# Cross attention's unit becomes a head pair with all four query tiles, and the left keys multiply a block-diagonal V

## The reference

```python
x = x + tanh(g_xattn[0]) * xattn(layernorm(x), ctx_1024, ctx_1024, mask)   # x: 2 x 512 x 256, ctx: 2 x 1024 x 256
# xattn: 16 heads of 64
dots = einsum('bhid,bhjd->bhij', heads(q @ Wq), heads(k @ Wk)) * 64 ** -0.5
dots = where(mask, -finfo.max, dots)                    # True is masked
out = einsum('bhij,bhjd->bhid', softmax(dots), heads(v @ Wv)) @ Wo + bo
x = x + tanh(g_ffn[0]) * ffn(layernorm(x))
# ffn: 8 experts of 256 x 256, gelu; each row takes the result of the expert with the largest gate
```

## Time and profile before

| | us |
|---|---|
| median of 3 runs | 241.98 (241.69 to 244.35) |
| the profiled execution | 242.49 |
| its span, first to last instruction | 240.7 |
| batch 0: first scores to Wo projection | 38.10 to 101.29 |
| batch 1: first scores to Wo projection | 127.29 to 180.84 |

### The profile page before, as it was taken

One profiled execution on the slowest core, in us unless ns is written; L12 is line 12 of the kernel. 1 busy time (PEld: TensorE's weight loads), 2 busy tenths in 40 slices (PEclk: granted clock), 3 DMA queues, 4 the chain that ended last, 5 costly groups with the idle time before them and its releaser, 6 DMA issues.

```text
span 240.7 us, 4102 instructions
## 1 busy us (share of the span) xinstructions
PE 217.7 (90%) x1316; PEld 145.8 (61%) x1316; DVE 134.3 (56%) x537; ACT 112.5 (47%) x386; POOL 90.5 (38%) x96
## 2 busy tenths in 40 slices
PE   0499999999999999999999799999999999959960
PEld 0334394456555544488894356565568899948950
DVE  0797424678878722325227777788883435345520
ACT  2101443877887721301234868778844034525420
POOL 5000710555544591000001657755483000776450
PEclk9999999999999999999999999999999999999995
DMA  3990658999990000091000100240000000235011
GB/s 113 365 394 26 183 234 252 331 317 313 233 316 13 0 3 1 0 297 52 3 1 0 46 3 22 62 143 0 0 3 1 3 0 0 82 112 162 31 49 30
DMA packets 21250, 25.24 MB, mean 105 GB/s; under 512 B 1875, under 2 KB 19805, under 8 KB 21088
## 3 DMA queue, kind: packets, MB, share of 16 engines
q1 hardware_dynamic: 19200, 22.58, 30.4%
q0 software_dynamic: 1152, 2.12, 2.6%
q10 hardware_dynamic: 864, 0.15, 0.3%
HBM read 14.21 MB, written 11.68 MB: 108 GB/s over the span
## 4 chain that ended last, share of the span: by engine, by line
PE 68%; issue 12%; DMA 6%; DVE 5%; POOL 4%; ACT 3%; POOLq 0%; DVEq 0%
PE s_bank L1491 11%; PE s_bank L1531 10%; PE bank L1560 8%; PE bank L1563 7%; PE bank L1450 6%; PE bank L1544 5%; PE s_bank L1588 4%; PE s_bank L1776 3%; PE bank L1545 3%; PE bank L1548 3%; DMA oT<-sorted_rows 2%; PE bank L1571 2%; PE bank L1787 2%; DMA rows<-in_x_dram 2%; POOL sorted_rows L537 2%
## 5 line engine op out<-in xcount | busy, mean ns | idle before, releaser
L563 POOL TENSOR_TENSOR probs<-probs,r_col 128x768 f32<-128x768 f32 x32 | 46.9, 1466 | 86.5 <-DVE r_col L1148 86.5
L717 ACT ACTIVATE probs<-probs,negm_run 128x192 f32<-128x192 f32 x128 | 57.1, 448 | 19.5 <-DVE negm_run L1173 19.5
L1173 DVE CUSTOM_DVE_ANT_0 probs<-s_bank,maskneg 128x192 f32<-128x192 f32 x128 | 39.5, 348 | 8.6 <-PE s_bank L1531 8.6
L1491 PE MATMUL s_bank<-xnT,wq_sb 128*128 128x512 f32 x64 | 31.7, 644 | 1.2 <-ACT xnT L670 0.6
L1182 DVE COPY pT<-bank 128x512 f32<-128x512 f32 x32 | 22.1, 691 | 13.6 <-PE bank L1545 13.6
L1531 PE MATMUL s_bank<-k_sb,q_sb 64*128 64x192 f32 x256 | 29.5, 349 | 0.0
L1450 PE MATMUL bank<-wo_sb,oT 128*128 128x256 f32 x128 | 28.7, 380 | 0.0
L1450 PEld LDWEIGHTS bank<-wo_sb,oT 128*128 128x128 f32 x128 | 23.9, 190 | 3.9 <-issue 0.9
L1531 PEld LDWEIGHTS s_bank<-k_sb,q_sb 64*128 64x128 f32 x256 | 20.0, 186 | 9.0 <-issue 7.9
L717 ACT ACTIVATION_READ_ACCUMULATOR probs<-probs,negm_run 128x1 f32 x128 | 24.1, 188 | 0.0
L1491 PEld LDWEIGHTS s_bank<-xnT,wq_sb 128*128 128x128 f32 x64 | 12.6, 206 | 16.4 <-issue 15.0
(11 more groups left out here) (141 smaller groups left out, 288.5 us busy)
## 6 DMA issues: line engine op xcount, KB each, us to landing
sorted_rows<-empty_row SPq DMA_DIRECT2D x8, 1040.0 KB, 13.3
oT<-in_L_ffn_W_dram SPq DMA_DIRECT2D x1, 2048.0 KB, 17.6
q_sb<-in_L_ffn_W_dram SPq DMA_DIRECT2D x1, 2048.0 KB, 8.4
oT<-sorted_rows SPq DMA_DIRECT2D x1, 1040.0 KB, 6.6
oT<-sorted_rows SPq DMA_DIRECT2D x8, 130.0 KB, 2.2
rows<-in_x_dram SPq DMA_DIRECT2D x2, 512.0 KB, 7.8
wq_sb<-in_L_xattn_Wq_dram SPq DMA_DIRECT2D x1, 1024.0 KB, 8.3
mask_sb<-in_mask_BxSxS_bk_dram SPq DMA_DIRECT2D x2, 512.0 KB, 9.9
```

The lines of the kernel that those rows point to most:

```text
L563: nc.gpsimd.tensor_tensor(part, part, r_col[:, u % PB].rearrange("p i h -> p (i h)") .unsqueeze(2).broadcast_to([P, 4, keys]), ALU.mult).t ...
L717: last = nc.scalar.activation(window_part(u, i, h), window_part(u, i, h), ACT.Exp, bias=negm_run[at], scale=-1.0, accum_out=l_run[at])
L1173: nc.vector.tensor_tensor_reduce(window_part(u, i, h), s_bank[u % 2][:, h, i * CK:i * CK + WK], maskneg[:, q, 0:WK], -SCALE, LARGEST, ALU. ...
L1491: last = nc.tensor.matmul(bank[m % 4], wq_sb[:, c, m * P:(m + 1) * P], xnT[:, c, b * N:(b + 1) * N], start=(c == 0), stop=(c == DC - 1))
```

## The change

The unit on PE, for everything behind the scores, is now a head pair with all four query tiles, eight a batch. PE does both scores of the next pair, then `values(m - 1)`, then twelve transposes, to banks 4 and 6 (head 0's wide and the left block of either half) and 5 (head 1's wide of both). The left half of `v_sb` is zeroed once by POOL, and the left V is copied to its two diagonal blocks (64 x 64 for a pair): one matmul of 128 x 128 against 512 columns then does both heads' left keys, and four of 128 x 64 against 256 columns add the wide ones, all in bank 7. `pT` holds one pair. DVE copies banks 4 and 6 and takes bank 7 in one copy; ACT copies bank 5, whole. Scatters follow multiplies 1 (two), 3 and 5. In batch 1's last pair `values(6)` comes ahead of the filled-in chunks. DVE takes half of the left V copy, which was all ACT's. The branch for other masks changes only in line numbers and counts.

```diff
+        pair_pT = pT[:].rearrange("p a h k n -> p (a h k n)")[:, 0:3 * 2 * CK].rearrange("p (s t n) -> p s t n", s=3, t=2)
+        pair_bank = (4, 6, 5)
...
-            return (v_sb[:, 0, 0:512], v_sb[:, 0, 512:1024], v_sb[:, 1, 0:512])[v], bank[(4, 6, 7)[v]]
+            return v_sb[:, 0, v * 512:(v + 1) * 512], bank[(4, 6)[v]]
+        v_left = v_sb[:, 1, :].rearrange("p (m h d) -> p m h d", h=2, d=DH)
+        def left_v_dst(h):
+            return v_left[head_rows[h], :, h, :], bank[7][head_rows[h], :].rearrange("p (m d) -> p m d", d=DH)
...
+            nc.gpsimd.memset(v_sb[:, 1, :], 0.0).then_inc(left_zero, 1)
...
-                if u == 0:
+            def sort_first_batch(u, first_scatter=1):
+                if u == first_scatter:
                     pool.wait_ge(s_empty, 16 * CH)
                     pool.wait_ge(place_ready, 1)
                     for q in range(2):
                         scatter(q)
-                elif u in (4, 6):
-                    scatter(u // 2)
+                elif u in (first_scatter + 2, first_scatter + 4):
+                    scatter((u - first_scatter) // 2 + 1)
...
-            def window_pT(b, u):
-                act.wait_ge(first.ptrans_ready, b * 2 * PER + (2 * u + 2))
-                if u >= 2:
-                    act.wait_ge(first.o_ready, b * PER + (u - 1))
-                nc.scalar.copy(pT[:, u % 2, 1, 0, :], bank[5][:, 0:2 * P]).then_inc(first.pT_act, 1)
+            def pair_pT_wide(b, m):
+                act.wait_ge(first.ptrans_ready, 3 * (b * M + m) + 3)
+                if m >= 1:
+                    act.wait_ge(first.o_ready, b * M + m)
+                nc.scalar.copy(pair_pT[:, 2].rearrange("p t n -> p (t n)"), bank[pair_bank[2]]).then_inc(first.pT_act, 1)
...
-                for u in range(AHEAD):
+                act.wait_ge(first.v_ps, b * 3 + 1)
+                nc.scalar.copy(*window_v_dst(0)).then_inc(first.v_act, 1)
+                for u in range(2):
                     window_exp(b, u)
-                    act.wait_ge(first.v_ps, b * 3 + (2 * u + 1))
-                    nc.scalar.copy(*window_v_dst(2 * u)).then_inc(first.v_act, 1)
-                for u in range(PER):
-                    if u + AHEAD < PER:
-                        window_exp(b, u + AHEAD, (0,))
+                act.wait_ge(first.v_ps, b * 3 + 3)
+                nc.scalar.copy(*left_v_dst(0)).then_inc(first.v_act, 1)
+                for m in range(M):
+                    if m + 1 < M:
+                        for u in (2 * m + 2, 2 * m + 3):
+                            window_exp(b, u)
                     else:
-                        fill(u + AHEAD - PER)
-                    window_pT(b, u)
-                    if u + AHEAD < PER:
-                        window_exp(b, u + AHEAD, (1,))
-                fill(2)
-                fill(3)
+                        fill(0)
+                    pair_pT_wide(b, m)
+                for k in range(1, 4):
+                    fill(k)
...
-            def window_pT(b, u):
-                dve.wait_ge(first.ptrans_ready, b * 2 * PER + (2 * u + 1))
-                if u >= 2:
-                    dve.wait_ge(first.o_ready, b * PER + (u - 1))
-                nc.vector.tensor_copy(pT[:, u % 2, 0].rearrange("p t n -> p (t n)"), bank[4]).then_inc(first.pT_dve, 1)
+            def pair_pT_left(b, m, j):
+                dve.wait_ge(first.ptrans_ready, 3 * (b * M + m) + 1 + j)
+                if m >= 1:
+                    dve.wait_ge(first.o_ready, b * M + m)
+                nc.vector.tensor_copy(pair_pT[:, j].rearrange("p t n -> p (t n)"), bank[pair_bank[j]]).then_inc(first.pT_dve, 1)
+            def pair_o(b, m):
+                dve.wait_ge(first.o_ready, b * M + m + 1)
+                nc.vector.tensor_copy(oT[:, b, m, :], bank[7]).then_inc(first.o_dve, 1)
...
-                for u in range(AHEAD):
+                for u in range(2):
                     window_max(b, u)
-                    also(f"v{u}")
-                    if u == 0:
-                        dve.wait_ge(first.v_ps, b * 3 + 2)
-                        nc.vector.tensor_copy(*window_v_dst(1)).then_inc(first.v_dve, 1)
-                        take_sum(first, b * PER, 0, l_run)
-                for u in range(PER):
-                    ahead = u + AHEAD
-                    if ahead < PER:
-                        window_max(b, ahead, (0,))
-                        take_sum(first, b * PER, ahead - 1, l_run)
-                        window_max(b, ahead, (1,))
+                also("v0")
+                take_sum(first, g, 0, l_run)
+                dve.wait_ge(first.v_ps, b * 3 + 2)
+                nc.vector.tensor_copy(*window_v_dst(1)).then_inc(first.v_dve, 1)
+                also("v1")
+                take_sum(first, g, 1, l_run)
+                dve.wait_ge(first.v_ps, b * 3 + 3)
+                nc.vector.tensor_copy(*left_v_dst(1)).then_inc(first.v_dve, 1)
+                for m in range(M):
+                    if m + 1 < M:
+                        for u in (2 * m + 2, 2 * m + 3):
+                            window_max(b, u)
                     else:
-                        if ahead == PER:
-                            take_sum(first, b * PER, PER - 1, l_run)
-                        fill(ahead - PER)
-                    window_pT(b, u)
-                    if u >= 1:
-                        take_o(first, b * PER, u - 1, b)
-                    also(u)
+                        fill(0)
+                    if m >= 1:
+                        pair_o(b, m - 1)
+                    if m + 1 < M:
+                        take_sum(first, g, 2 * m + 2, l_run)
+                    for j in range(2):
+                        pair_pT_left(b, m, j)
+                    if m + 1 < M:
+                        take_sum(first, g, 2 * m + 3, l_run)
+                    also(m)
+                fill(1)
+                pair_o(b, M - 1)
                 fill(2)
-                take_o(first, b * PER, PER - 1, b)
                 fill(3)
...
-                if k == 2:
-                    first_rows(range(5, 7))
+                if k == 0:
+                    first_rows(range(2, 3))
...
-                if where in (PER - 5, PER - 4):
-                    first_rows(range(where + 5 - PER, where + 6 - PER))
-                elif where == PER - 2:
-                    first_rows(range(2, 5))
+                if where == M - 2:
+                    first_rows(range(2))
+                elif where == M - 1:
+                    first_rows(range(3, 6))
...
-                def transposes(u):
-                    pe.wait_ge(first.pn_ready, g + (u + 1))
-                    if u >= 1:
-                        pe.wait_ge(first.pT_act, g + u)
-                        pe.wait_ge(first.pT_dve, g + u)
-                    tiles = window_probs(u).rearrange("p (i t k) -> p i t k", i=2, t=3)
-                    for i in range(2):
-                        nc.tensor.transpose(bank[4][:, i * P:(i + 1) * P], tiles[:, i, 0], ident[:])
-                        last = nc.tensor.transpose(bank[4][:, CK + i * P:CK + (i + 1) * P], tiles[:, i, 1], ident[:])
+                def transposes(m):
+                    if m >= 1:
+                        pe.wait_ge(first.pT_act, b * M + m)
+                        pe.wait_ge(first.pT_dve, b * PER + 2 * m)
+                    for j in range(2):
+                        u = 2 * m + j
+                        pe.wait_ge(first.pn_ready, g + (u + 1))
+                        tiles = window_probs(u).rearrange("p (i t k) -> p i t k", i=2, t=3)
+                        to, wide = bank[pair_bank[j]], bank[pair_bank[2]]
+                        for i in range(2):
+                            nc.tensor.transpose(to[:, i * P:(i + 1) * P], tiles[:, i, 0], ident[:])
+                            last = nc.tensor.transpose(to[:, CK + i * P:CK + (i + 1) * P], tiles[:, i, 1], ident[:])
+                        last.then_inc(first.ptrans_ready, 1)
+                        for i in range(2):
+                            last = nc.tensor.transpose(wide[:, j * CK + i * P:j * CK + (i + 1) * P], tiles[:, i, 2], ident[:])
                     last.then_inc(first.ptrans_ready, 1)
-                    for i in range(2):
-                        last = nc.tensor.transpose(bank[5][:, i * P:(i + 1) * P], tiles[:, i, 2], ident[:])
-                    last.then_inc(first.ptrans_ready, 1)
-                def values(u):
-                    m = u // 2
-                    pe.wait_ge(first.pT_act, g + (u + 1))
-                    pe.wait_ge(first.pT_dve, g + (u + 1))
-                    if u >= 2:
-                        pe.wait_ge(first.o_dve, g + u - 1)
-                    to = bank[6 + u % 2]
-                    for h in range(2):
-                        nc.tensor.matmul(to[head_rows[h], 0:CK], v_sb[:, 0, (h * M + m) * DH:(h * M + m + 1) * DH],
-                                         pT[:, u % 2, h, 0, :], start=True, stop=False)
```

(43 more changed lines are left out.)

37 lines of the change are left out of this document (20 added, 17 removed).

## The result

The changed kernel takes 234.84 us (median of 4 executions, 232.89 to 235.93) against 242.28 for the kernel before on the same chip: ratio 0.9665, 95% interval 0.9623 to 0.9707. Ratios and intervals are given as recorded: they leave out executions in a slower state that kernels sometimes run in (for scatter_old too few others remain), and they are not the quotients of the medians. The forecast was 231.4 us with a range of 229.4 to 236.5. The direction, the mechanism and the place of the gain were right; the time came out 3.4 us above the forecast.

The account below looks back on a forecast made before the run. The prediction took PE's own group period to bound attention: fewer shape changes and altered waits save 5.1 in batch 0 and 5.6 in batch 1, together 10.7, so 242.49 becomes 231.8 profiled, median 231.4 us; range 229.4 to 236.5.

Parts of the forecast that it names:

- rival A: Wide values: the two heads stop overlapping at the new wait for ACT's copy, +0.43 a pair, 238.3 us; chance 0.11.
- Block diagonal booked at 0: Left values on PE: one block matmul saves no stream, 0.86 a pair either way, since the heads' passes already run side by side.
- 0.165 a change of shape: PE pair: each tile-shape change costs 0.165 us; four instead of eight save 0.66 a pair, 10.6 over 16 pairs.
- Second scores at once: A pair's second scores follow the first without a shape change of their own; if they paid one, 2.6 us less saved.
- rival B: The first pair's 0.6 wait for DVE's pT copies repeats in the other 14 pairs: +8.8, 240.2 us; chance 0.05.
- rival C: DVE becomes the bound, its copies slowed beside POOL's multiplies: 5.94 a pair at 1.35, 246.8 us; chance 0.03.
- V(0): Values of each batch's first pair: PE waits 0.6 for DVE's pT copies, lacking an earlier pair's values as cover.
- V(6) of batch 1: Values of pair 6 in batch 1's last iteration: no scores stand ahead, so PE waits 0.7 for pT copies.
- Batch 1 saves 5.6: Batch 1's attention: 5.3 + 0.4 + 1.2 - 0.6 - 0.7 = 5.6 us saved, the 1.2 being the wait on POOL's multiply.
- T(1): Transposes of pair 1; in batch 1 not wanted before 140, multiply 2 ending near 138.8, so the 1.2 wait goes.
- Behind each attention PE goes on without a wait, so the rest shifts: Stages after each attention: they start earlier by what the attention saves and lose none of it.
- 242.49 - 10.7: Whole kernel: profiled execution before less the sum of both batches' savings gives 231.8; the median 0.5 under it, 231.4 us.

Follow-up runs that it names:

- scatter_old: Changed kernel with the scatters back in their old places (two behind multiply 0, one each behind 4 and 6): batch 1's attention 50.73 us against 49.42; ratio not to be used.
- left_tiles: Changed kernel with the block-diagonal matmul undone into two side-by-side 64x64 matmuls of 512 columns: pair 4.98 us against 5.03, ratio 0.9644 to the kernel before.
- block_last: Changed kernel with the wide heads first and the block next to the transposes, three shape changes a pair: pair 4.88 us against 5.03, ratio 0.9594 to the kernel before.
- block_by_unit: Kernel before, order by unit kept, with only the block-diagonal left V, standing ahead of the transposes (six shape changes a pair): attentions 61.54 and 52.10 us, ratio 0.984.
- block_unit_first: Kernel before, order by unit kept, with the block-diagonal left V ahead of the wide heads (eight shape changes a pair): attentions 63.36 and 53.88 us, ratio 0.9928.
- best_late: Changed kernel with the block last in pairs 2 to 5 and one scatter behind each of multiplies 1, 3, 5, 7: 230.65 us, ratio 0.9488 to the kernel before.
- shape_more: Changed kernel with the block cut in two between the wide halves, five shape changes a pair: pair 5.18 us against 5.03, ratio 0.9818 to the kernel before.
- copies_first: Changed kernel with DVE copying both transposed tiles before the next pair's first reciprocal in each batch's first pair: attentions 57.98 and 49.63 us, ratio 0.9622 to the kernel before.
- best_mixed: Changed kernel with the block last in pairs 1 to 5 and one scatter behind each of multiplies 1, 3, 5, 7: ratio 0.9541 to the kernel before.

## Why the prediction was right or wrong, point by point

The mechanism was right and is shown. That the median falls into the stated range is in part luck: 234.84 lies above the 234.5 at which the forecast's own range ended, and is covered only because the range was widened to half of rival A, which did not happen.

- **Block diagonal booked at 0: right**, and a hair generous. It costs 0.05 a pair (left_tiles: 4.98 against 5.03).
- **0.165 a change of shape, eight changes to four: right.** With two matmuls for the left values the pair is 4.98, exactly the sum's 4.98; the changed kernel's 5.03 is that plus the block's 0.05. Counted as doses, in kernels that all have the block, a change comes to 0.15; where the difference of 0.015 lies is open. The alternative named as the one that would break most, a cost for starting any group, fell with block_last and with the pair block_by_unit and block_unit_first, where the number of groups stays and the number of changes does not.
- **Second scores at once, no cost to the wide heads' wait: right.** Sixteen score passes take 1.50, and the wide heads 1.02 with the wait between them. Rival A fell.
- **DVE, ACT and POOL have room: right.** DVE is busy 33.04 of 38.79 and 42.88 of 49.41. Rivals B and C fell: PE waits for DVE's pT copies three times in the whole kernel, not once a pair.
- **V(0) waits 0.6 a batch, V(6) of batch 1 0.7: right.** V(0) waits 0.52 and 0.69 (row 132.47 above), V(6) 0.59. The 0.4 waits on the V copies are gone, as said.
- **Zeroing hidden: right.** On POOL's timeline it ends at 4.65, before DVE's first work at 5.78:

```profile
3.71 0.94 POOL L534 MEMSET v_sb<- 128x1024 f32 x1
```

- **Batch 0 saves 5.1: right** (5.1).
- **Batch 1 saves 5.6: wrong, 4.1.** The failed step is "multiply 2 then ends near 138.8, T(1) is not wanted before 140". I set the first scatter right behind multiply 1, though the earlier trace rows has the figure in its brackets: 1.66 of idle time ahead of the scatter. I took all of that for the wait on the place table; a pause of that length stands ahead of the first scatter whoever it is put down to (1.63 and 1.64 above, with "issue" in place of DVE). Multiply 2 ends at 134.85, on the forecast's scale (this stage began 6.02 later before) 140.9 and not 138.8, and pair 1's transposes could have begun at 134.55. So they wait 0.39, and their second half 0.48 more: 0.87. With one scatter less in that place the stage takes 48.28. Of the rest, 0.4 are the block's 0.05 in eight pairs, and some 0.2 are what PE loses beyond a wait's length when it starts again. Batch 0 pays the 0.05 in six pairs, and makes it good: its wait at V(0) is 0.1 smaller, and in each of its last two pairs the block follows a q projection of its own shape and is 0.14 ahead of what left_tiles needs there. So its 5.1 is right with two small errors that cancel.
- **"Behind each attention PE goes on without a wait, so the rest shifts": wrong by +1.1 us in the profiled execution.** Between the attentions it held (26.00 both times). In the rest, PE waits 1.74 for rows read back by DMA, and then the granted clock falls to its 1.2 GHz level for 3.4 us. First the kernel before, which waits 2.29 in that place, then the changed one:

```profile
215.47 0.77 PE L1765 MATMUL s_bank<-ident,xnT 128*128 128x128 f32 x4 [2.29 <-DVE xnT L1106]
```

```profile
204.69 0.79 PE L1795 MATMUL s_bank<-ident,xnT 128*128 128x128 f32 x4 [1.74 <-DVE xnT L1120]
205.59 1.44 PE L1806 MATMUL s_bank<-k_sb,q_sb 128*128 128x128 f32 x8
...
210.42 1.06 PE L1806 MATMUL s_bank<-k_sb,q_sb 128*128 128x128 f32 x8
```

```profile
206.30:209.70 3.40, 3.40 (x16) 3.31 (x16) 1.37 (x4) 1.39 (x5) 2.61 (x3) 0.50 0.51 131
209.70:213.10 3.40, 3.40 (x26) 3.10 (x26) 1.78 (x5) 1.50 (x5) 1.39 (x2) 1.00 0.41 123
```

  The last view is busy time by stretch, the clock third from the end: 16 matmul records in 3.4 us at the lower level, 26 at the full one. Where the stretch is absent (scatter_old, best_late) the rest takes 58.74 and 58.29. That the change brings it about is not shown, and these two, which go by pairs as well, speak against it; on the second chip every kernel profiled had such a stretch of 6.8 or 10.2 us, block_by_unit with the old order too, and before waited longer there at a full clock.
- **The start, -0.9, was not foreseen.** The q projections are the same in both kernels, but the clock reached its full level at 15.2 us and not at 16.9. Over the eleven kernels the first scores come between 37.0 and 38.3, in no order of their edits. It is no gain of the change.
- **"242.49 - 10.7", the time outside the span held fixed: wrong.** It was 1.7 to 1.9 us in 37 executions of before and 13 of the two kernels in the old order, but in the changed kernel 2.0 to 2.4 in five executions and 3.8 to 4.4 in five. It does not go with the order by pairs alone: it was 1.8 to 2.2 in all 14 executions of left_tiles, block_last and shape_more, and 3.6 to 5.0 in at least one of each of the other five kernels by pairs. By its span the changed kernel is 9 us faster on either chip; by its median 7.4 and 7.2. What these 0.3 to 2.5 us are is open: nothing in the profile lies there.
- **Slips in the sums.** In rival B 14 x 0.6 is 8.4 and gives 239.8, not 8.8 and 240.2. The upper end of the forecast's own range, 231.4 with the second scores paying 2.6, is 234.0 and not 234.5. Neither moves the forecast.

The profiled execution took 235.93 where the sum gave 231.8. The terms of this 4.1 are 1.5 (attention 1), 1.1 (rest) and 2.5 (outside the span), less 0.9 (start). Only the first is shown to be the change's; of the last three none was priced in the sum, and the 0.9 that helped was luck. The median missed by 3.4.

## What to carry to other kernels

Count the changes of tile shape on TensorE before counting passes: order the groups so that neighbours share a shape, and take larger units, so that each change is paid once for more work; side-by-side tiles already hide what a block-diagonal trick would merge. Put the group that covers a late copy first in the few places where that copy is late, and nowhere else. When work is moved on an in-order queue, move the idle time in front of it too: brackets that name a releaser may hold a pause that stays when the releaser is long done.

## What the runs showed of the hardware that was not expected

- The first indirect scatter of the program starts 1.63 to 1.69 us behind the multiply ahead of it in eight of the twelve kernels, the kernel before and the changed one among them, and 1.84 to 1.91 in left_tiles, block_last, copies_first and best_mixed; the three after it, behind a multiply or behind one another, 0.15 to 0.31. What GpSimd does in that time, and why it comes in two lengths, the profile doesn't show.
- DVE's normalisation of a routed row block (SBUF to SBUF, 128x256) takes 0.40 alone (in the kernel before, at 168.47) and 0.91 when GpSimd multiplies or adds at the same time; VectorE's copies from PSUM beside the same multiplies stay at 0.67 to 0.69. The row of the changed kernel, DVE's timeline, POOL busy throughout:

```profile
162.89 2.73 DVE L1120 TENSOR_SCALAR wk_sb<-oT 128x256 f32<-128x256 f32 x3
```

  The Trainium skill, GPSIMD Engine Reference, Specifications, says that the two share SBUF interfaces, with contention in some of VectorE's modes. This row agrees that there is contention, though it does not show the mode; the copies that rival C rested on are not hit.
